# The mixing product of a two-layer metaformer kernel, cut into two row tiles and added by one instruction

## The reference, cut to what matters

```python
idx = jnp.argmax(sim, axis=1)
sim = sim * mask                       # one of M = 4 clusters for a head and token
agg = (einsum('bmn,bnc->bmc', sim, value2) + value_centers) / (sum(sim) + 1.0)
out = jnp.einsum('bmc,bmn->bnc', agg, sim)
...
return _conv1x1(out, proj_w, proj_b)   # and x = x + this
```

## Time and profile before

| | |
|---|---|
| median of 3 executions | 8480.61 us (8476.2 to 8494.93) |
| span of the profiled execution | 8464.2 us, from its first to its last instruction |
| between the two | 16.4 us, counted as start and end of the execution |
| instructions in the profile | 429416 |
| busy share of the span | PE 88%, DVE 80%, PEld 71%, ACT 58%, POOL 31% |
| granted TensorE clock, mean | 0.944 of 2.4 GHz |

### The profile page before, as it was taken

The page is one execution under the profiler, slowest core; times in us unless marked ns, Lnnn a source line. Parts: engine busy times, 40 slices in busy tenths (PEclk is TensorE's granted clock), DMA queues, the critical chain, the costliest instruction groups (busy, mean ns, idle before and its releaser), DMA issues.

```text
span 8464.2 us, 429416 instructions
## 1 busy us (share of the span) xinstructions
PE 7468.5 (88%) x172050; PEld 6008.7 (71%) x172050; DVE 6788.1 (80%) x22260; ACT 4867.1 (58%) x9750; POOL 2630.1 (31%) x5004
## 2 busy tenths in 40 slices
PE   6899989998999999998999999998999999996555
PEld 4777777777777777777777777777777777775332
DVE  3677777777888888888888888888888888887566
ACT  2455555554666666665666656666666656665545
POOL 1333333333333333332333323333333333332112
PEclk7899999999999999999999999999999999997766
DMA  2111112212222222222222222222222222221211
GB/s 59 41 45 44 44 49 51 51 51 52 65 62 65 66 61 62 66 68 59 62 67 61 66 59 64 63 67 63 64 62 65 63 64 62 65 63 55 64 60 51
DMA packets 193345, 501.77 MB, mean 59 GB/s; under 512 B 33508, under 2 KB 67108, under 8 KB 191468
## 3 DMA queue, kind: packets, MB, share of 16 engines
q1 hardware_dynamic: 191692, 476.75, 20.7%
HBM read 228.84 MB, written 169.93 MB: 47 GB/s over the span
## 4 chain that ended last, share of the span: by engine, by line
PE 59%; DVE 24%; issue 9%; ACT 5%; DMA 1%; DVEq 0%; SPq 0%; ACTq 0%; POOL 0%; POOLq 0%
PE scores_x L703 8%; DVE maxes L1579 6%; PE bank L662 6%; PE flipped L725 5%; PE bank L665 3%; PE pv L753 3%; PE scores_x L645 3%; DVE shifted L1587 3%; PE misc L782 3%; PE pv L747 2%; PE bank L673 2%; PE bank L975 2%; PE flipped L1019 2%; DVE z8c L1871 2%; PE flipped L1002 2%
## 5 line engine op out<-in xcount | busy, mean ns | idle before, releaser
L2061 POOL TENSOR_TENSOR vrest<-vstage,vmask 96x384 f32<-96x384 f32 x512 | 434.4, 848 | 4247.2 <-ACT vstage L1209 4247.2
L1579 DVE TENSOR_REDUCE maxes<-scores_x 128x6 f32<-128x864 f32 x1024 | 1076.8, 1052 | 577.1 <-PE scores_x L703 574.7
L703 PE MATMUL scores_x<-keys,queries 64*64 64x144 f32 x24576 | 1033.5, 298 | 190.2 <-ACT queries L1197 102.2
L703 PEld LDWEIGHTS scores_x<-keys,queries 64*64 64x64 f32 x24576 | 752.0, 136 | 409.4 <-issue 375.3
L665 PE MATMUL bank<-xn,wq 97*32 97x64 f32 x24576 | 910.5, 224 | 76.6 <-issue 75.5
L1587 DVE TENSOR_TENSOR shifted<-scores_x,maxes 128x768 f32<-128x768 f32 x1024 | 969.6, 947 | 0.0
L662 PE MATMUL bank<-xt,wq 97*32 97x64 f32 x24576 | 886.1, 223 | 69.7 <-issue 66.6
L662 PEld LDWEIGHTS bank<-xt,wq 97*32 97x32 f32 x24576 | 754.5, 112 | 249.3 <-issue 183.9
L725 PE MATMUL flipped<-ident,shifted 128*128 128x128 f32 x6144 | 858.1, 276 | 0.2 <-ACT vstage L1209 0.2
L665 PEld LDWEIGHTS bank<-xn,wq 97*32 97x32 f32 x24576 | 770.6, 110 | 87.2 <-issue 85.5
L1197 ACT ACTIVATE queries<-bank 128x512 f32<-128x512 f32 x768 | 456.0, 594 | 592.6 <-PE bank L665 592.4
(11 more groups left out here) (203 smaller groups left out, 17151.3 us busy)
## 6 DMA issues: line engine op xcount, KB each, us to landing
keys<-kst SPq DMA_DIRECT2D x768, 99.0 KB
x_in<-x_dram SPq DMA_DIRECT2D x130, 396.0 KB
xn_kept<-xn SPq DMA_DIRECT2D x128, 388.0 KB, 2.4
later<-xn_kept SPq DMA_DIRECT2D x128, 388.0 KB, 3.3
x_tok<-tok_dram SPq DMA_DIRECT2D x128, 384.0 KB, 3.3
x_kept<-x SPq DMA_DIRECT2D x128, 384.0 KB, 2.3
later<-x_kept SPq DMA_DIRECT2D x128, 384.0 KB, 3.4
out_dram<-later SPq DMA_DIRECT2D x128, 384.0 KB, 2.5
```

The costliest lines, as they stand in the source:

```text
L703: last = mm(score[e][64 * j:64 * j + 64, g * NKEY:(g + 1) * NKEY], queries[64 * e:64 * e + 64, g, w, :], keys[64 * e:64 * e + 64, g, :, WS ...
L1579: V.tensor_reduce(maxes[:, p % 2, :, :], sc, AX.X, ALU.max).then_inc(max_ready.sem, 1)
```

## The change

The 128-row product with 384 columns becomes two products of 64 rows with 192 columns each, put on two row tiles of the PE array (`tile_position` (0, 0) and (64, 0)). Rows 0 to 63 hold the first two of the four token tiles, whose results are the first 192 columns; rows 64 to 127 the other two. Row tile r writes to bank r, u chooses the columns in it. All four matmuls stand at the place of the former `mix(n, 0)`, wait for `hc_evac` 6, and DVE adds the whole with one instruction of 128 x 768 numbers before `best_of(n)`. The counts of `mix_ready` and `mixed` go from 2 to 1 a step. `bank` becomes one PSUM tensor of two banks so that one instruction can read both.

```diff
@@ attend, PE
                 if on.c1:
                     if on.c2:
-                        pe.wait_ge(hc_evac.sem, hc_evac.at(n, 5))
-                    mix(n, 0, fill)
+                        pe.wait_ge(hc_evac.sem, hc_evac.at(n, 6))
+                    mix(n, fill)
                 if ahead:
                     make_queries(n + 1, 2)
                 flip_heads(1)
                 if ahead:
                     make_queries(n + 1, 3)
-                if on.c1:
-                    if on.c2:
-                        pe.wait_ge(hc_evac.sem, hc_evac.at(n, 6))
-                    mix(n, 1, fill)
                 project(1)
@@ mix, PE
-            def mix(n, u, dst):
+            def mix(n, dst):
                 pe.wait_ge(st_ready.sem, st_ready.at(n, 1))
-                mm(dst[u][:, 0:4 * C], simw_t[:, u, :], mix_w[:, :, :].rearrange("p t c -> p (t c)"),
-                   start=True, stop=True).then_inc(mix_ready.sem, 1)
+                for u in range(2):
+                    for r in range(2):
+                        rows = slice(64 * r, 64 * r + 64)
+                        last = mm(dst[r][:, 2 * C * u:2 * C * (u + 1)], simw_t[rows, u, :],
+                                  mix_w[rows, 2 * r:2 * r + 2, :].rearrange("p t c -> p (t c)"),
+                                  start=True, stop=True, skip_group_check=True, tile_position=(64 * r, 0))
+                last.then_inc(mix_ready.sem, 1)
@@ attend, DVE
                 if on.c1:
-                    mix(n, 0, par, fill)
+                    mix(n, par, flipped)
                 if on.b:
                     best_of(n)
-                if on.c1:
-                    mix(n, 1, par, fill)
                 residual(1)
@@ mix, DVE
-            def mix(n, u, par, src):
-                dve.wait_ge(mix_ready.sem, mix_ready.at(n, u + 1))
+            def mix(n, par, src):
+                dve.wait_ge(mix_ready.sem, mix_ready.at(n, 1))
                 dve.wait_ge(xc_loaded, (n - LAG_C) * 16 + 16)
-                V.tensor_tensor(xc[par][:, 4 * u:4 * u + 4, :], xc[par][:, 4 * u:4 * u + 4, :],
-                                src[u][:, 0:4 * C].rearrange("p (t c) -> p t c", c=C), ALU.add
+                part = xc[par].rearrange("p (u r t) c -> p u r (t c)", u=2, r=2)
+                V.tensor_tensor(part, part, src[:, :, 0:4 * C].rearrange("p r (u c) -> p u r c", u=2), ALU.add
                                 ).then_inc(mixed.sem, 1)
@@ drain, PE and DVE
-                    mix(n, 0, work)
-                    mix(n, 1, work)
+                    mix(n, work)
...
-                    mix(n, 0, par, work)
-                    mix(n, 1, par, work)
+                    mix(n, par, bank)
```

More of the change, by code:

```diff
@@ L220, in build @@
         keys_g = keys[:, :, :, :].rearrange("p g a b -> p g (a b)")
-        bank = [ctx.enter_context(nc.psum_tensor(f"bank{i}", [128, 512], F32)) for i in range(2)]
-        work = bank
+        bank = ctx.enter_context(nc.psum_tensor("bank", [128, 2, 512], F32))
+        work = [bank[:, i, :] for i in range(2)]
         scores_x = ctx.enter_context(nc.psum_tensor("scores_x", [128, 2, 512], F32))
@@ L316, in build @@
         st_ready = signal("st_ready", 1, LAG_C)
-        mix_ready = signal("mix_ready", 2, LAG_C)
-        mixed = signal("mixed", 2, LAG_C)
+        mix_ready = signal("mix_ready", 1, LAG_C)
+        mixed = signal("mixed", 1, LAG_C)
         c_bn = signal("c_bn", 2, LAG_C + 1)
@@ L796, in attend @@
                         if on.c2:
-                            pe.wait_ge(mixed.sem, mixed.at(n - 1, 2))
+                            pe.wait_ge(mixed.sem, mixed.at(n - 1, 1))
                         make_values(n, 1, fill)
@@ L1035, in strip @@
                     pe.wait_ge(hc_evac.sem, hc_evac.at(n, 6))
-                    pe.wait_ge(mixed.sem, mixed.at(n, 2))
+                    pe.wait_ge(mixed.sem, mixed.at(n, 1))
                     flip_z(n, 0)
@@ L1838, in add_gathered @@
                                 ).then_inc(gather_added.sem, 1)
-            def mix(n, u, par, src):
-                dve.wait_ge(mix_ready.sem, mix_ready.at(n, u + 1))
+            def mix(n, par, src):
+                dve.wait_ge(mix_ready.sem, mix_ready.at(n, 1))
                 dve.wait_ge(xc_loaded, (n - LAG_C) * 16 + 16)
-                V.tensor_tensor(xc[par][:, 4 * u:4 * u + 4, :], xc[par][:, 4 * u:4 * u + 4, :],
-                                src[u][:, 0:4 * C].rearrange("p (t c) -> p t c", c=C), ALU.add
+                part = xc[par].rearrange("p (u r t) c -> p u r (t c)", u=2, r=2)
+                V.tensor_tensor(part, part, src[:, :, 0:4 * C].rearrange("p r (u c) -> p u r c", u=2), ALU.add
                                 ).then_inc(mixed.sem, 1)
             def stats_c(n, par):
-                dve.wait_ge(mixed.sem, mixed.at(n - 1, 2))
+                dve.wait_ge(mixed.sem, mixed.at(n - 1, 1))
                 for t in range(TILES):
```

## The result

The changed kernel takes 8596.9 us (median of 4, 8577.4 to 8619.07); the kernel before, beside it on the same chip, 8486.14 us (8476.2 to 8494.93). The ratio is 1.0124, 95% interval 1.0100 to 1.0148: **slower**, and outside the range of 8405 to 8494 us. The profiled execution has a span of 8608.9 us, 144.7 more than before, at a mean granted clock of 0.921 instead of 0.944. That is more than the 110.8 us between the medians. The changed kernel's executions last 1.8 us longer than their spans, so the 16.4 us that stand above as start and end of an execution were for the most part chance: the execution that was profiled before was faster than the median, while the one profiled after (8610.7 us) was slower than its own.

The account below looks back on a forecast made before the run. PE at each strip's end was taken as bound by its streamed program, swallowing most savings. Strips -10 us and last 16 short steps -9 us made -19 us off the 8480.6 us median: 8461 us, range 8405 to 8494.

Parts of the forecast that it names:

- the 16.4 us that stand above as start and end of an execution: Whole kernel: the profiled span of 8464.2 us lies 16.4 below the median of 8480.6, from which the saving was taken.
- The tiles' overlap and the first place, 0.84 us: Strips' mixing on PE: four matmuls, two tiles side by side, cost 0.84 us at the first place.
- The 1.67 us bound: Same place: 1536 columns at 1.09 ns each cost 1.67 us if nothing overlaps; that rival had chance 0.09.
- DVE: Mixing's addition: two of 546 ns become one near 947 ns, 0.15 us less work, off the chain; cost nothing.
- the wait for `hc_evac` 6: Mixing on PE in strips: the wait comes two query blocks earlier; cost nothing.
- A saving comes through at 20%: End of each strip: of 0.84 us PE work saved, some 20%, 0.17 us, comes back; the rest becomes issue idle.
- The comparison of the earlier trace with the earlier trace: Strips without against with mixing: issue idle 2.01 against 0.67 us a strip; base of the 20%.
- The 1.34 us between them: Issue idle that goes away when mixing adds 1.68 us of PE work; about 80% of mixing's time.
- The borders: Rival in strips: program 8 instructions longer, borders move to a worse place; 0.25 us a strip, 8496 us and up; chance 0.11.
- "The clock is no matter here": PE in the strips: granted clock 0.99 of 2.4 GHz, so no clock term was counted.
- "In the 18 short steps the chain isn't at the mixing; 0": The 18 short steps before the last 16: the change is worth 0 there.
- The last 16 short steps, 0.54 us each: Mixing alone on the chain: matmuls 1.29 us for 2.57, addition done 0.54 us earlier; 16 steps, 9 us.

Follow-up runs that it names:

- e15: Changed kernel with the same four matmuls, each of all 128 rows and without row tiles, in strips and all short steps; 8531.1 us, ratio 1.0103.
- e8: Kernel before with half the columns (192 for 384) in the strips' mixing products, every instruction in its place; 8471.8 us, ratio 0.9999 to 1.0032.
- e11: Kernel before with the change in the last 16 short steps only, plus 158 dummy instructions at the start of PE's program; 8546.1 us, ratio 1.0055 to 1.0103.
- e7: Kernel before with the change in the last 16 short steps only; 8453.5 us, ratio 0.9980 to 1.0012.
- e3: Changed kernel with full 128-row products in all 34 short steps, still one place and one addition; 8565.9 us, ratio 1.0111.
- e4: Changed kernel doing the four 64-row products twice in the first 18 short steps; 8551.8 us, ratio 1.0077 to 1.0125.
- e6: Changed kernel with full products in the first 18 short steps and 102 dummy instructions ahead of the loop; 8485.0 us, ratio 1.0024.
- e10: Kernel before with the change in the last 16 short steps only, plus 110 dummy instructions at the start; 8528.2 us, ratio 1.0027 to 1.0072.
- e12: Kernel before with the change in the last 16 short steps only, plus 208 dummy instructions at the start; 8487.6 us, ratio 0.9972 to 1.0032.
- e17: Changed kernel with full products in the first 18 short steps, 166 dummies at the start, no row tiles in strips or last 16 steps; 8484.7 us, ratio 1.0046.
- e1: Kernel before with 158 dummy semaphore instructions on PE once, ahead of the loop over strips 50 to 113; 8565.7 us, ratio 1.0066 to 1.0166.

## Why the prediction was wrong, point by point

1. **The tiles' overlap and the first place, 0.84 us: right.** It takes 0.850 us; without tiles the same matmuls take 1.497 us (e15). The 1.67 us bound was too high, because the price of 1.09 ns a column holds a fixed part: 0.842 us for 768 columns and 0.522 for 384 (e8) make 0.83 ns a column and 0.20 us besides. With these the tiles leave 0.85 - 0.20 = 0.65 us for 1536 columns, as much as 780 take at 0.83 ns: full overlap, on this estimate. The Trainium skill ("TensorE: Matmul & The Clock Gate", Part 3) gives 3.07-fold for four row tiles, an estimated 77% of full overlap; with two tiles this case shows no such loss.
2. **DVE, the wait for `hc_evac` 6: right.** The addition takes 945 ns; L1001 waits for ACT's copy for 0.2 us, all 94 strips together.
3. **A saving comes through at 20%: right in size, rather less, but not by its reasoning.** In e8 0.10 of 0.64 us comes through, with the loop unchanged. The comparison of the earlier trace rows with the earlier trace rows doesn't show it, though: a strip without mixing has 2658 instructions, so its borders pass through every place in turn, while those of the 14 strips with mixing stayed at 118 to 160 (and 256 and 512 more). The 1.34 us between them mix the borders' place with the mixing, and that the 20% came out near e8's 16% was in part luck. The reading of the issue idle as the program's arrival is borne out: it lies at distances of 256 instructions and moves with dummies. The rule of the Trainium skill ("Runtime: NRT & Kernel Launch", Instruction fetch mechanics), by which a crossing is mostly hidden, does not hold in this stretch: in the strip shown a crossing took 1.66 us.
4. **The borders, the first failed step.** I priced a strip with issue idle of 1.3 us and gave the case in which borders move 0.11. Measured: 2.16 us a strip. The new strip is 6 instructions longer, not 8, since two waits went with the second place; its length (2819, against 11 x 256 = 2816) could have been counted beforehand. The rival's price was too low as well: 0.25 us a strip, where e11 against e7 shows 72 / 64 = 1.1 us. Its mechanism was the right one, and it had 0.11.
5. **"The clock is no matter here", the second.** It was 0.99 in those strips, but for the kernel before; with the shorter product it is 0.97, and half-speed time in the loop went from 137 to 208 to 263 us (four kernels with the tiles at these borders). e15, without the tiles, has 113 us, and its loop is 19 to 40 us shorter. Of the changed kernel's 61 to 82 us in the loop some 45 are the borders and the rest goes with the falls.
6. **"In the 18 short steps the chain isn't at the mixing; 0", the third.** True of the chain, not of the time: +36.1 us, because PE's work on the chain behind it ran at 1.2 GHz for more of the time (clock 0.54). e3, e4, e6 and e15 show it four ways. Over the short steps before the change the clock was 0.70 already, and the prediction left that out; the earlier trace rows is of the full strips alone.
7. **The last 16 short steps, 0.54 us each: right in the sum, 9 us.** 9.1 to 9.6 us in all, and it needs the tiles (e3: none of it). The product was mis-sized, 1.61 us instead of 1.29, but DVE was free only at about the same time, as forecast, and no longer waits for it; in the step shown 0.46 us came of it.

What stays open: why the places of e10 and e11 are bad and that of e12 is not (that they are is shown, the arithmetic of each wait isn't); the exact split between borders and clock, since loops of the same kernel differ by 20 us; why e17 gained nothing; and why the clock falls behind one long wait and not behind the next.

## What to carry to other kernels

Where an engine's program is streamed in pieces through a stretch of very small instructions, count the instructions of a loop body before editing it. A length near a whole number of pieces holds the borders at one place, good or bad, for the whole loop. Read a result only with the borders' place held equal: dummies at the start, where the engine waits anyway, do that, and moved this kernel between -0.4% and +0.8%. Work taken from PE pays only if it lies on the chain and PE keeps its clock without it: in a step half idle, look at the granted clock of the matmuls behind the edit before counting the saving. An edit that helps in one stage (here the last 16 steps) can be made in that stage alone.

## What the runs showed of the hardware

- PE does not run on through its own program: in the query matmuls it stood for 0.2 to 1.7 us at many of the borders of 256 instructions, and these waits took up 0.47 of 0.64 us that a shorter product had freed (e8).
- Of the 30 late falls of the clock in the changed kernel's loop 27 came soon behind a long wait at such a border, as behind the 1.66 us in strip 60; without the row tiles (e15) there were 5 late falls in all.
- Doubling a product made 17 short steps 34 us shorter (426.8 to 392.8, e4), with a granted clock of 0.67 instead of 0.54.
- 158 dummy semaphore instructions on PE took 24.4 us, 0.15 us each (e1).
